# Self-attention's tail taken by batch entry, and cross-attention's masked maxima in groups of four heads

## The reference

```python
# self-attention (L1_attn): query, key from low-rank and rotary parts
attn = jnp.einsum('bhqd,bhkd->bhqk', query, key) / scale
attn = jax.nn.softmax(attn, axis=-1)
out = jnp.einsum('bhqk,bhkd->bhqd', attn, value)
return out.transpose(0, 2, 1, 3).reshape(b, s, d_model) @ Wo_w + Wo_b
# cross-attention (L1_xattn) to 512 context tokens, with a mask of (2, 256, 512)
q = jnp.einsum('bse,ehd->bhsd', query, Wq) + bq[:, None, :]
logits = jnp.einsum('bhsd,bhtd->bhst', q, k)
logits = jnp.where(mask[:, None, :, :], jnp.float32(-100000000.0), logits)
score = jax.nn.softmax(logits, axis=-1)
attn = jnp.einsum('bhst,bhtd->bhsd', score, v) / jnp.sqrt(jnp.float32(D_HEAD))
out = jnp.einsum('bhsd,hdo->bso', attn, Wo) + bo
```

## Time and profile before

| | |
|---|---|
| median of 3 runs | 486.89 us |
| the profiled execution | 487.24 us |
| its span, first to last instruction | 485.1 us |
| mean granted clock of TensorE | 0.976 |
| busy: PE, DVE, ACT, POOL | 423.2, 306.9, 206.8, 145.0 us |

### The profile page before, as it was taken

How to read it: one execution, slowest core, us unless ns; L and a number is a source line. 1 busy time by engine, 2 the same in 40 slices (tenths; PEclk the granted TensorE clock), 3 DMA queues, 4 the chain that set the end, 5 groups by cost and what they waited for, 6 DMA issues and landing times.

```text
span 485.1 us, 7466 instructions
## 1 busy us (share of the span) xinstructions
PE 423.2 (87%) x2852; PEld 269.4 (56%) x2860; DVE 306.9 (63%) x712; ACT 206.8 (43%) x268; POOL 145.0 (30%) x138
## 2 busy tenths in 40 slices
PE   5867989999999999789999878698578999997984
PEld 5665645444555556556778355344434445556874
DVE  4789976676666665416213587953697777338754
ACT  1765623333333322153323388574154445546320
POOL 3226647877777774100302200000200000005111
PEclk9989999999999999999999887999998999999998
DMA  8611000000023110610440430000000000010000
GB/s 306 263 34 59 1 0 2 1 1 1 0 84 134 45 45 0 219 51 1 110 59 17 62 40 3 3 3 1 0 1 3 1 3 1 2 34 1 1 1 22
DMA packets 7791, 19.58 MB, mean 40 GB/s; under 512 B 1862, under 2 KB 3686, under 8 KB 7238
## 3 DMA queue, kind: packets, MB, share of 16 engines
q1 hardware_dynamic: 7756, 19.10, 13.5%
HBM read 17.26 MB, written 1.15 MB: 38 GB/s over the span
## 4 chain that ended last, share of the span: by engine, by line
PE 60%; DVE 21%; ACT 5%; issue 5%; POOL 5%; SPq 2%; DMA 1%; DVEq 0%; POOLq 0%
PE ps L1373 58%; DVE ps L1170 3%; DVE mx_a L1174 2%; POOL big L588 2%; SPq L445 1%; ACT big L768 1%; DVE big L983 1%; DVE ps L978 1%; POOL rstd L521 1%; PE ps L1385 1%; POOL big L595 1%; PE ps L1753 1%; DMA ident<-in_ident 1%; DVE big L1332 1%; DVE attn_w L917 1%
## 5 line engine op out<-in xcount | busy, mean ns | idle before, releaser
L1373 PE MATMUL ps<-big,late 128*32 128x256 f32 (+4 forms) x792 | 99.8, 383 | 11.8 <-DVE mid L909 4.5
L1373 PEld LDWEIGHTS ps<-big,late 128*32 128x32 f32 (+3 forms) x800 | 38.9, 117 | 52.0 <-issue 22.0
L794 ACT ACTIVATE big<-ps 128x1024 f32<-128x1024 f32 x48 | 48.9, 1023 | 40.3 <-PE ps L1373 39.8
L1373 PE MATMUL ps<-late,big 128*128 128x128 f32 (+1 forms) x448 | 64.1, 275 | 1.6 <-DVE mx_x L1170 1.3
L519 POOL TENSOR_SCALAR vareps<-meanvar 128x4 f32<-128x4 f32 (+2 forms) x11 | 2.6, 232 | 197.4 <-DVE meanvar L886 193.7
L732 ACT ACTIVATE big<-ps 128x1024 f32<-128x1024 f32 x32 | 32.8, 1024 | 65.3 <-PE ps L1373 58.9
L1373 PEld LDWEIGHTS ps<-late,big 128*128 128x128 f32 (+1 forms) x448 | 44.7, 152 | 25.2 <-issue 21.0
L588 POOL TENSOR_TENSOR big<-big 128x512 f32<-128x512 f32 x32 | 41.0, 1283 | 28.2 <-DVE big L1055 28.2
L1170 DVE CUSTOM_DVE_ANT_0 ps<-ps,big 128x512 f32<-128x512 f32 x64 | 42.6, 717 | 10.0 <-PE ps L1373 6.9
L1055 DVE TENSOR_SCALAR big<-big 128x1024 f32<-128x1024 f32 x32 | 27.6, 864 | 33.3 <-ACT big L732 33.3
L1373 PE MATMUL ps<-ident 128*128 128x128 f32 x232 | 30.3, 293 | 5.7 <-DMA ident<-in_ident 5.7
(11 more groups left out here) (255 smaller groups left out, 691.8 us busy)
## 6 DMA issues: line engine op xcount, KB each, us to landing
attn_w<-in_w_x SPq DMA_DIRECT2D x1, 2560.0 KB, 13.1
big<-parts_kx SPq DMA_DIRECT2D x18, 128.0 KB
late<-in_w_up SPq DMA_DIRECT2D x1, 2048.0 KB, 8.9
late<-in_w_dn SPq DMA_DIRECT2D x4, 512.0 KB, 3.9
attn_w<-in_w_up SPq DMA_DIRECT2D x1, 1024.0 KB, 5.9
attn_w<-in_w_dn SPq DMA_DIRECT2D x1, 1024.0 KB, 7.9
parts_kx<-ctx_r SPq DMA_DIRECT2D x1, 768.0 KB, 3.3
rowv<-in_rowv SPq DMA_DIRECT2D x1, 576.0 KB, 4.1
```

Source lines behind the costliest of these rows:

```text
L794: nc.scalar.activation(ex1[:, n % 3, :].rearrange("p (r n) -> p r n", r=2), ps[:, 2 * (n % 2):2 * (n % 2) + 2, :], ACT.Exp, scale=scale).t ...
L1373: return nc.tensor.matmul(o, lhsT, rhs, start=start, stop=stop, skip_group_check=shared)
```

## The change

Three things change together. First, self-attention's tail is taken by entry: entry 0's turning, division and projection stand at passes 9, 11 and 13 of its loop, its sum and norm at 13 and 15; what is left of it, and entry 1's tail (in banks 0 and 1), stand behind the loop, and entry 1's norm and query matmul stand between the first rows of cross-attention. "post3" becomes "post3_0" and "post3_1". Second, cross-attention's queries are split and gathered by entry: DVE copies only the first four heads of entry 0; the other twelve heads go by nine DMAs, entry 1's sixteen by twelve, from SP's list. Spreads take two heads, one bank: those of entry 0 stand ahead of the loop in banks 4 and 5, those of entry 1 are slots of passes 2 to 9, copied by ACT. Third, the maxima are taken in groups of four heads (8 rows): 16 rows and one group ahead of the loop in banks 6, 7, 2 and 3, and then three rows a pass over passes 0 to 15; groups stand at passes 0, 3, 6, 8, 11, 14 and 16. ACT negates and copies a group's maxima from PSUM, and POOL splits them. In ACT's list the copies of pass n - 1's slots stand behind the exponential of pass n.

```diff
-        AHEAD = {"a": 24, "x": 24}
+        GROUP = {"a": 8, "x": 4}
+        AHEAD = {"a": 24, "x": 16}
+        ROW_RATE = {"a": 2, "x": 3}
+        FIRST_BANKS = {"a": (0, 1, 2, 3), "x": (6, 7, 2, 3)}
+        def groups(L):
+            return B * H // GROUP[L]
+        def heads_of(L, k):
+            b, i = divmod(k, H // GROUP[L])
+            return b, GROUP[L] * i
         def row_steps(L):
-            return 2 * HB * KEYS[L] // 512
+            return 2 * GROUP[L] * KEYS[L] // 512
         def row_of(L, m):
             k, i = divmod(m, row_steps(L))
-            return k, i % 2, HB * (k % 2) + i // 2 * (512 // KEYS[L])
+            b, h = heads_of(L, k)
+            return b, i % 2, h + i // 2 * (512 // KEYS[L])
...
+            step, rows = ROW_RATE[L], row_steps(L)
+            m = AHEAD[L] + step * n
+            slots = [("max", k) for k in range(groups(L)) if m - step < (k + 1) * rows <= m]
+            if L == "x" and 2 <= n < 2 + H // 2:
+                slots.append(("spread", H // 2 + n - 2))
+            return slots + [("row", i) for i in range(m, min(m + step, groups(L) * rows))]
...
-            banks = [i % 4 for i in range(len(first) - 2)] + [6, 7]
+            banks = [FIRST_BANKS[L][i % 4] for i in range(len(first) - 2)] + [6, 7]
             return ([(None, s, bank) for s, bank in zip(first, banks)]
                     + [(n, s, 6 + i % 2) for i, (n, s) in enumerate(later)])
...
-        TURNED = {"a": (10, 14), "x": (21, 30)}
-        BESIDE = {"aT": 22, "y": 23, "xT": 26, "router": 27}
+        def first_in(L, banks):
+            return [s for n, s, bank in placed_slots(L) if n is None and bank in banks][-1]
+        TURNED = {"a": 9, "x": 21}
+        BESIDE = {"a": {"aT": 11, "y": 13}, "x": {"aT": 22, "y": 23, "xT": 26, "router": 27}}
+        TAIL = {"a": ((6, 7), (0, 1)), "x": ((6, 7), (6, 7))}
+        def spreads_x(m):
+            return [0, 1] if m < 0 else [2 + m // 2] if m % 2 and 2 + m // 2 < H // 2 else []
+        SECOND = {"xT": 1, "q": 3, "parts": 5}
...
+            def gather_queries(b, fs):
+                for i in range(PARTS):
+                    sp.wait_ge(S["x_q_parts"], PARTS * b + i + 1)
+                    for f in fs:
+                        sp.dma_start(fours[32 * i:32 * i + 32, f, b * T:(b + 1) * T],
+                                     parts1["qx"][32 * f:32 * f + 32, i, b * T:(b + 1) * T]
...
-            spread_max("a")
-            spread_max("x")
+            for k in range(groups("a")):
+                spread_max("a", k)
+            gather_queries(0, (1, 2, 3))
+            spread_max("x", 0)
+            sp.wait_ge(S["x_fours_dma"], 16 * 3 * PARTS)
+            gather_queries(1, (0, 1, 2, 3))
+            for k in range(1, groups("x")):
+                spread_max("x", k)
...
+            def minus_parts(k):
+                m, done = k % 2, S["x_nm_done"]
+                src, parts = nm[0:GROUP["x"], m, :], nmp[0:GROUP["x"], m, :, :]
+                pool.wait_ge(S["x_nm_ps"], k + 1)
+                if k >= 2:
+                    pool.wait_ge(S[f"x_nm_stack{m}"], 16 * PARTS * (k // 2))
+                nc.gpsimd.tensor_copy(parts[:, 0, :], src).then_inc(done, 1)
+                pool.wait_ge(done, PARTS * k + 1)
+                link(nc.gpsimd.tensor_tensor(src, src, parts[:, 0, :], ALU.subtract))
+                nc.gpsimd.tensor_copy(parts[:, 1, :], src).then_inc(done, 1)
+                pool.wait_ge(done, PARTS * k + 2)
+                nc.gpsimd.tensor_tensor(parts[:, 2, :], src, parts[:, 1, :], ALU.subtract
+                                        ).then_inc(done, 1)
+            for k in range(groups("x")):
+                minus_parts(k)
...
+            def spread_x(n, bank):
+                b, h = divmod(2 * n, H)
+                act.wait_ge(S["x_spread_ps"], n + 1)
+                nc.scalar.activation(qs[:, h:h + 2, b * T:(b + 1) * T],
+                                     ps[:, bank, :].rearrange("p (h t) -> p h t", h=2), ACT.Copy
+                                     ).then_inc(S["x_spread"], 1)
+            def minus_max(k, bank):
+                act.wait_ge(S["x_mT_ps"], k + 1)
+                if k >= 2:
+                    act.wait_ge(S["x_nm_done"], PARTS * (k - 1))
+                nc.scalar.activation(nm[0:GROUP["x"], k % 2, :], ps[0:GROUP["x"], bank, 0:T], ACT.Copy,
+                                     scale=-1.0).then_inc(S["x_nm_ps"], 1)
+            def attend_x():
+                for n in spreads_x(-1):
+                    spread_x(n, 4 + n % 2)
+                for (kind, i), bank in slots_beside("x", None):
+                    if kind == "max":
+                        minus_max(i, bank)
+                        continue
+                    for n in spreads_x(i):
+                        spread_x(n, 4 + n % 2)
+                    if i == SECOND["xT"]:
+                        half_cols("a", 1)
+                for n in range(B * (H // 4) * KEYS["x"] // P):
+                    exp_late("x", n)
+                    for (kind, i), bank in slots_beside("x", n - 1) if n else ():
+                        if kind == "spread":
+                            spread_x(i, bank)
+                        elif kind == "max":
+                            minus_max(i, bank)
...
+            def a_summed(b):
+                dve.wait_ge(S["a_y_ps"], b + 1)
+                dve.wait_ge(S["res_ready"], 4)
+                link(nc.vector.tensor_tensor(half(summed, b), ps[:, TAIL["a"][b][1], 0:T],
+                                             half(resid, b), ALU.add))
+                statistics(f"post3_{b}", summed[:, 2 * b:2 * b + 2, :])
+            def a_scaled(b):
+                scaled(f"post3_{b}", summed[:, 2 * b:2 * b + 2, :], x[:, 2 * b:2 * b + 2, :])
...
+                    if n == BESIDE["a"]["y"]:
+                        a_summed(0)
+                    if n == B * (H // 4) * KEYS["a"] // P - 1:
+                        a_scaled(0)
+                    kept("a", n)
+                    if n == TURNED["a"]:
+                        normed_rows("a", 0, 1.0)
+                normed_rows("a", 1, 1.0)
+            def query_parts(b):
+                cols = slice(b * T, (b + 1) * T)
+                dve.wait_ge(S["qk_ps"], 7 + b)
+                split(ps[:, TAIL["a"][b][1], 0:T], [parts1["qx"][:, i, cols] for i in range(3)],
+                      cv[:, 0, cols], S["x_q_parts"], PARTS * b, ALU.add, v("bq"))
+            def attend_x(factor):
+                for (kind, i), bank in slots_beside("x", None):
+                    if kind == "row":
+                        row_max("x", i, bank)
+                        if i == SECOND["xT"]:
+                            a_scaled(1)
+                        if i == SECOND["parts"]:
+                            query_parts(1)
+                for n in range(B * (H // 4) * KEYS["x"] // P):
+                    for (kind, i), bank in slots_beside("x", n):
+                        if kind == "row":
+                            row_max("x", i, bank)
...
+            def used(L, slot):
+                kind, i = slot
+                if kind == "row":
+                    pe.wait_ge(S[f"{L}_redmax"], i + 1)
+                elif kind == "spread":
+                    pe.wait_ge(S["x_spread"], i + 1)
+                elif L == "a":
+                    pe.wait_ge(S["a_nm_done"], PARTS * i + 2)
+                else:
+                    pe.wait_ge(S["x_nm_ps"], i + 1)
...
+            def spread_x(n, bank):
+                b, u = divmod(n, H // 2)
+                f, i = divmod(u, 2)
+                if b:
+                    pe.wait_ge(S["x_fours_dma"], 16 * 7 * PARTS)
+                elif f:
+                    pe.wait_ge(S["x_fours_dma"], 16 * 3 * PARTS)
+                else:
+                    pe.wait_ge(S["x_fours"], 1)
+                for r in range(2):
+                    ins = mm(ps[:, bank, r * T:(r + 1) * T], sel_s[:, 2 * i + r, :],
+                             fours[:, f, b * T:(b + 1) * T])
+                ins.then_inc(S["x_spread_ps"], 1)
+            def fill_slot(L, slot, bank):
+                kind, i = slot
+                before = before_in_bank(L, slot)
+                if before:
+                    used(L, before)
+                if kind == "row":
+                    rows(L, i, bank)
+                elif kind == "max":
+                    max_cols(L, i, bank)
+                else:
+                    spread_x(i, bank)
...
+            def attend_x():
+                total = B * (H // 4) * KEYS["x"] // P
+                half_cols("a", 0)
+                out_rows("a", 1, (H // 4 - 1,))
+                queries(0)
+                attended_cols("a", 1)
+                attended_rows("a", 1)
+                idle_work(2, 8)
+                pe.wait_ge(S["a_o_sb"], 2 * (H // 4))
+                for n in spreads_x(-1):
+                    spread_x(n, 4 + n % 2)
+                pe.wait_ge(S["mask_done"], 2)
```

(56 more changed lines are left out.)

520 lines of the change are left out of this document (233 added, 287 removed).

## The result

The changed kernel took 501.66 us (median of 4 runs, 500.43 to 502.52), the kernel before 487.06 on the same chip: ratio 1.029 with a 95% interval of 1.0267 to 1.0313. It is 2.9% slower, 3.7 us above the predicted 498.0. The profiled execution has a span of 500.5 us against 485.1.

A forecast was written before the change was run, and what follows sets the result against it. TensorE, holding 60% of the chain, was taken as the bound, with VectorE's maxima before the loop. First logits 12.2 us earlier and the loop 23.0 longer gave +10.8 on 487.24, 498 us; range 489 to 508.

The forecast's parts named there:

- what a pass costs: Cross-attention loop, passes 0 to 15: bank waits make passes 2.98, 3.88, 3.66 or 4.66 us, 59.3 us in all.
- The loop ended: End of cross-attention's loop: forecast at 443.4 against 432.5 before, 10.9 us later.
- The first logits: Cross-attention's first logits matmul: at 355.9, within 354 to 359, 12.2 us before the old 368.06.
- GpSimd's four operations: Split of group 0's negative maxima ahead of the first logits: 0.65 us each, 2.6 in all, at most 1.5 each.
- The clock: TensorE's granted clock in the new loop: rows decide neither way; its fall was only a rival, chance 0.15.
- rival B: Clock falls in the loop: about 2 us a pass, 514 through eight spread passes, 506 through half; chance 0.15.
- the sixteen behind them: Loop from pass 16, at 417.0, to its end, fifteen passes behind it: 26.4 us.
- The first masked maximum: Start of cross-attention's row maxima on VectorE: near 340.6, 11.4 us earlier than the old 352.07.
- TensorE's idle ahead of the gathered spread: Sign after row 1, ahead of the loop: TensorE idle 3 us or more, ended by the gather DMA.
- TensorE's idle in the loop: Sign in the loop: some 21 us of idle put down to VectorE's maxima and ScalarE's spread copies.
- A (the waits don't bind): Second and third rows of passes 0 to 15 don't wait: 37.6 us for 59.3, time 476; 489 if half true; together 0.09.
- C (GpSimd late everywhere): Each of the seven later groups makes its logits wait, 3 us each, 21 us in all: 519; chance 0.03.

The follow-up runs named there:

- values_between: Changed kernel with values(n) issued on TensorE behind the first two entries of each list in passes 0 to 16, ahead of the rest: 489.32 us, ratio 1.0037.
- both_orders: Changed kernel with values(n) behind the pass's first two entries on TensorE and ScalarE's copies ahead of exp(n+1): 487.40 us, ratio 0.9979.
- late_spreads: Changed kernel with spread copies 2 to 7 of entry 0 two rows later each, ahead of the loop: 498.31 us, ratio 1.0212.
- busy_sized: Changed kernel plus unread matmuls: 9 behind row 9, 4 behind row 13, 5 before logits(0), one behind each first two entries of passes 0-3: 498.61 us, ratio 1.0222.
- groups_of_eight: As two_rows_a_pass on the changed kernel, with maxima in groups of eight heads in place of four: 497.14 us, ratio 1.0179.
- two_rows_a_pass: Changed kernel with 24 rows ahead of logits(0) in place of 16, then two rows a pass in place of three: 492.97 us, ratio 1.0092.

## Why the prediction was right, and where its sizes were off

**The sign and the mechanism** were right: the front wins, the loop loses more. The largest term, what a pass costs, was right to 0.13: 3.01 for 2.98 (three rows), 3.76 for 3.88 (a spread), 3.53 for 3.66 (maxima), 4.55 for 4.66 (both), at full clock. That TensorE's waits behind two banks are the cause, and do not only agree with the sum, is shown by values_between and both_orders, which change nothing but the order and take the loss away (2.4 us of it by the clock that came back with the order). One sum is a little off: the terms listed for a spread give 1.87 us, not 1.90, and so 3.85 for its pass.

The loop ended at 447.88, 4.5 later than predicted. In order:
- **The first logits**: 358.07 for 355.9. 1.8 of it stood there before any changed line ran: a like copy ahead of self-attention's maxima starts at 288.06, before at 286.27, while at 159 the two differ by 0.11. It is not the change's doing: in the twelve executions of kernels with the change, the first of these copies starts anywhere from 285.6 to 287.8 (287.5 here, 285.7 before). Between 159 and there the granted clock was 0.90 and 0.92 over 190 to 210, before 1.00; but late_spreads had 0.95 and 0.88 and its copy starts at 285.9, so what makes the difference is not shown. The other 0.4 is the sum of small terms: self-attention's end +0.2, from the first query part to the copied maxima +0.5 (the nine DMAs took 0.59 each and 1.81, as taken), GpSimd's four operations -0.2 (2.34 for 2.6), the last DMA -0.1.
- **The clock** was the step that was mis-sized. I gave its fall a chance of 0.15 as a rival and nothing in the sum; it came, but briefly: the first two logits took 3.37 for 1.76 (+1.6), passes 3 and 4 together 10.68 for 8.54 (+2.1). Eight slow passes (rival B) it never was: from 384 on the clock was 1.00, with the same pauses. The Trainium skill, "TensorE: Matmul & The Clock Gate", section "A second HAM failure mode: psum-queue depth-cycling", says that short idles between groups of matmuls on cycling banks can swing the clock. busy_sized agrees, as filling the idles kept it at 1.00 from 352 on. But passes 5 to 15 cycle in the same way and ran at full clock, so the rule names the risk and not the size.
- **The passes** at full clock were 0.1 shorter than predicted, -1.0 together; the sixteen behind them -0.4.

1.8 + 0.4 + 1.6 + 2.1 - 1.0 - 0.4 = 4.5. Without the part ahead of the change the loop's end was forecast 2.7 us too early.

**The fillers** are a term that the sum lacked. In the seam the kernel before runs matmuls that nobody reads, 12 and then 10 (two records each). The change takes these out and puts in 8; "The change" shows only the latter (`idle_work(2, 8)`). Before, and then after:

```profile
338.49 2.84 PE L1373 MATMUL ps<-ident 128*128 128x128 f32 x24
345.39 2.40 PE L1373 MATMUL ps<-ident 128*128 128x128 f32 x20
```

```profile
340.40 1.95 PE L1508 MATMUL ps<-ident 128*128 128x128 f32 x16
```

Before, the clock was 1.00 from 336 to 360, then fell, and was back at 1.00 from 368 on, when the first logits ran; here it fell near 355 and was low in the first logits. busy_sized shows that 18 fillers in the front and 8 in the first passes keep it at 1.00 there and in passes 3 and 4. No run puts the old 22 back alone, so how much of the clock's 3.7 us their absence explains is open.

**The signs.** The first masked maximum came at 343.89, not near 340.6: 1.8 of the 3.3 is the late start above, and then the eight fillers ran to 342.35 ahead of the spread, whose input was gathered by 341.30. It cost nothing at the first logits, as rows 0 and 1 were reduced by 345.2 and row 2 stood until the gather landed at 346.15. So TensorE's idle ahead of the gathered spread was 2.3 us and not 3 or more. TensorE's idle in the loop is listed with 15.4 us, where some 21 were named; a matmul's shown span is longer than the time after which the next can start, so a stall is listed short (pass 1: 0.64 for 0.80).

**The rivals.** A (the waits don't bind) was wrong for this kernel and not far off as a price: I put a loop without them at 476 (its sum takes the turns of four groups, but six stand in passes 0 to 15, so 0.4 more), and the version in which TensorE hardly pauses measured 480.28, with 24 rows ahead of the loop. C (GpSimd late everywhere): its later groups made no logits wait.

## What to carry to other kernels

An earlier start is worth only what the next bound lets through: write out the next loop's queue, instruction by instruction, before adding a third use of a bank that has two. Where a wait must stay, put work that needs neither bank behind the second use and ahead of the third, and let the engine that frees the bank read it before its own long instruction. A pause that the order makes can also lower TensorE's clock, so measure the order first and the clock after it.

## What the runs showed that I had not expected

- GpSimd took 0.39 us for a cast and 0.66 for a subtraction of 4x256, and the same in groups_of_eight for 8x256: the number of partitions did not matter.
- A 128x128 float32 filler matmul took 0.233 us, two records each, in a queue of sixteen; the ten of the kernel before (2.40 us) would have told me.
- Eight more rows ahead of the loop (two_rows_a_pass) moved the first logits by only 3.2 to 3.6 us, against 5.2 by the price of a row: the logits need not wait for VectorE's last row. In the changed kernel they start just as it ends (358.07 and 358.00), there 2.0 us ahead of its end (361.09 and 363.1).
- The half clock of passes 3 and 4 came at the same passes in late_spreads, and in neither kernel a second time in the loop; why there, and not at passes 6 to 9 of the same kinds, stays open.
